# One slot's order on three engines: the exponential ahead of y's tanh, the decay matmul ahead of the gram products, z's gate first and gated y behind N

## The reference

```
y = silu(conv(xn @ W_qkvz))          # q, k, v ; z is taken from the projection, not convolved
beta = sigmoid(b); g = -exp(A_log) * softplus(a + dt_bias)
step: S = S*exp(g); delta = (v - k.S)*beta; S = S + k (x) delta; o = q.S
gated = o * silu(z); gated = rmsnorm(gated) * norm_w ; out = gated @ W_out
```

## Time and profile before

| | |
|---|---|
| median of 3 runs | 3296.51 us (3288.0 to 3297.0) |
| the profiled execution | 3288.43 us, span 3286.7 us |
| mean granted TensorE clock | 0.98 |
| busy, share of the span | PE 92%, weight loads 67%, DVE 71%, ACT 54%, POOL 49% |
| the delta rule's slots | from about 480 us to 2740 us without a break, a slot near 19.8 us |

### The profile page before, as it was taken

How to read it: one execution, slowest core, us unless ns; L and a number is a source line. 1 busy time by engine, 2 the same in 40 slices (tenths; PEclk the granted TensorE clock), 3 DMA queues, 4 the chain that set the end, 5 groups by cost and what they waited for, 6 DMA issues and landing times. The chain is left out here.

```text
span 3286.7 us, 70205 instructions
## 1 busy us (share of the span) xinstructions
PE 3032.7 (92%) x23017; PEld 2186.7 (67%) x23017; DVE 2336.3 (71%) x4933; ACT 1760.5 (54%) x5786; POOL 1621.3 (49%) x3745
## 2 busy tenths in 40 slices
PE   6997699999999999999999999999999999978998
PEld 4555367777767776777677667777776777765555
DVE  3443577777777777777777777777777777755776
ACT  4222466566666666566666666556665666532322
POOL 1000566666666666666666666666666666620000
PEclk9998799999999999999999999999999999987999
DMA  3000111111111111111111111121111111100000
GB/s 74 0 0 20 26 41 37 43 41 44 38 39 40 40 42 36 41 35 42 35 42 35 42 35 42 37 50 37 44 35 42 36 44 36 35 26 22 7 7 13
DMA packets 447056, 113.77 MB, mean 35 GB/s; under 512 B 350496, under 2 KB 445840, under 8 KB 446672
## 3 DMA queue, kind: packets, MB, share of 16 engines
q1 hardware_dynamic: 446672, 108.98, 14.8%
HBM read 63.85 MB, written 45.09 MB: 33 GB/s over the span
## 5 line engine op out<-in xcount | busy, mean ns | idle before, releaser
L876 ACT ACTIVATE raw<-bank 128x512 f32<-128x512 f32 x256 | 153.0, 598 | 433.8 <-PE bank L670 338.7
L467 POOL TENSOR_TENSOR Tb<-Tb,btmp 64x14 f32<-64x14 f32 (+6 forms) x896 | 317.3, 354 | 70.5
L1080 DVE SCALAR_TENSOR_TENSOR N<-ET,ty,bank 128x128 f32<-128x128 f32 x512 | 143.6, 342 | 272.6 <-POOL ET L409 272.6
L1134 DVE SCALAR_TENSOR_TENSOR conv<-raw,ckq,conv 128x512 f32<-128x512 f32 x384 | 308.1, 802 | 26.7 <-ACT conv L877 15.6
L1134 DVE SCALAR_TENSOR_TENSOR conv<-raw,cv,conv 128x512 f32<-128x512 f32 x384 | 312.1, 813 | 14.5 <-ACT conv L877 3.5
L463 POOL TENSOR_TENSOR btmp<-Bk,Tb 64x14 f32<-64x14 f32 (+6 forms) x896 | 274.6, 307 | 65.6
L670 PE MATMUL bank<-xnT,wkq 128*128 128x512 f32 x512 | 254.0, 620 | 42.5 <-ACT ET L831 19.2
L434 POOL TENSOR_TENSOR ty<-ty 128x4 f32<-128x4 f32 x128 | 40.0, 312 | 459.5 <-ACT sq_gat L864 459.5
L670 PE MATMUL bank<-xnT,wv 128*128 128x512 f32 x512 | 249.4, 610 | 11.6 <-issue 7.0
L739 PE MATMUL bank<-wout_h,gT 128*128 128x256 f32 x1024 | 247.8, 385 | 5.2 <-ACT gT L896 5.2
L525 PE MATMUL bank<-S,ykq 128*128 128x256 f32 x1024 | 242.9, 379 | 1.4 <-issue 1.4
(11 more groups left out here) (350 smaller groups left out, 7855.6 us busy)
## 6 DMA issues: line engine op xcount, KB each, us to landing
blk_n<-N SPq DMA_DIRECT2D x128, 256.0 KB, 2.8
Tp<-blk_t SPq DMA_DIRECT2D x128, 128.0 KB, 2.9
Wp<-blk_w SPq DMA_DIRECT2D x128, 128.0 KB, 2.9
wkq<-in_L_attn_W_qkvz_dram SPq DMA_DIRECT2D x32, 128.0 KB, 2.2
wv<-in_L_attn_W_qkvz_dram SPq DMA_DIRECT2D x16, 256.0 KB
Bk<-blk_n SPq DMA_DIRECT2D x64, 64.0 KB, 2.7
blk_t<-Tb SPq DMA_DIRECT2D x64, 64.0 KB, 2.5
blk_w<-Wb SPq DMA_DIRECT2D x64, 64.0 KB, 2.5
```

Source lines behind the costliest of these rows:

```text
L467: pool.tensor_tensor(Tb[:, j + 1:, 0:j], Tb[:, j + 1:, 0:j], tmp, ALU.subtract).then_inc(row_rdy, 1)
L876: act.activation(raw[h][:, j, :, 3:], bB[1 - j], ACT.Copy)
L1080: i = dve.scalar_tensor_tensor(out=N[t.c % RING][:, u, :], in0=ET[:, u, :], scalar=ty[t.c][:, CC, u:u + 1], in1=bB[3][:, u // 2, 0:P], op0 ...
L1134: dve.scalar_tensor_tensor(out=conv[h][:, j], in0=raw[h][:, j, :, k:k + 256], scalar=cw[:, j, k:k + 1], in1=conv[h][:, j], op0=ALU.mult, o ...
```

## The change

Nothing is added or removed; four functions or groups move within a slot. On PE the decay matmul, with its waits, goes ahead of the two gram matmuls, with theirs. On ACT y's tanh goes from first place to behind the exponential. On DVE z's gate goes from third place to first, and y's gate (`silu`) from fifth place to behind `strict`.

```diff
                 def front(s):
                     ...
                     i.then_inc(kq_tp, 1)
+                    pe.wait_ge(gtri_rdy, t.done())
+                    wait(pe, zz_rdy, t.done(4))
+                    ends(pe, s, araw_rdy, t, -1)
+                    pe.matmul(bank[1][:], m["gt"][:], gtri[:].rearrange("p u n -> p (u n)"), start=True,
+                              stop=True).then_inc(dt_mm, 1)
                     wait(pe, N_rdy, t.done(1))
                     wait(pe, attn_rdy, t.done(1))
                     for b in range(B):
                         i = pe.matmul(bB[3][:, b], chunk(y, t, 0, b), ...)
                     i.then_inc(gram_mm, 1)
-                    (the same five lines)
@@ ACT
                 def body(s):
-                    silu(s)
                     ztanh(s)
                     from_state(s)
                     xev64(s)
                     norms(s)
                     expo(s)
+                    silu(s)
                     normed(s)
@@ DVE
                 def body(s):
+                    gate(s)
                     accumulate(s)
                     rhs(s)
-                    gate(s)
                     xev16(s)
-                    silu(s)
                     add_w64(s)
                     add_w1(s)
                     strict(s)
+                    silu(s)
                     uscale(s)
```

More of the change, by code:

```diff
@@ L632, in front @@
                     i.then_inc(gram_mm, 1)
[L633 to L637, removed]
                 def values(s):
```

## The result

The changed kernel takes 3320.92 us (median of 5 runs, 3314.92 to 3324.07) against 3296.51 (5 runs, 3288.0 to 3299.77): ratio 1.0074, 95% interval 1.0056 to 1.0092, so about 24 us slower. The profiled execution took 3320.92 us, 32.5 more than the profiled one of before. The kernel before was timed 47 times more beside the experiments, with medians of 3289.0 to 3291.2 us, so the cost may be nearer to 30 us than to 24.

A forecast was written before the change was run, and what follows sets the result against it. PE, 95% busy, was taken as the bound, each slot set by the chain through ACT, POOL and DVE to apply. A 0, B +0.95 us over 60 pairs, 57 less 4 for zz, gave +53: 3340 us, range 3290 to 3366.

The forecast's parts named there:

- main case: Whole kernel: late blocks from the DMA still hold B slots, so it is slower, 3340 us, own range 3325 to 3362; chance 50.
- blocks early: Rival: Tb is ready 0.7 us sooner, B slots cost only +0.3 us; 3302 us, +5 to +30; chance 24 in 100.
- ACT without y's tanh in front: ACT, slot's front: squares come 1.21 us earlier, at 3.51 us after state_in; the exponential runs at 4.53.
- POOL in the A slot: With y's gate gone, POOL's last base_first instruction shortens from 1.23 us and derive starts at 4.80 instead of 6.01.
- y's gate behind N: DVE, A slot: N at 8.20, the gate adds 1.13 us before Us; state_in to apply 11.11 us against 11.19.
- The B slot: Transposes, 0.85 us late through x16's wait for Tp, now hold the squares; state_in to apply about 11.9 us against 10.94.
- N 1.2 us earlier: Sign on DVE: the prediction is wrong if N doesn't start 1.2 us earlier.
- Does s stay: Transposes' 0.85 us delay by late Tp in B stays: y's gate stretches base_rest by 0.95 to 1.1 of 1.21 gained.
- DVE held by POOL: DVE may lose 0 to 0.4 us where it starts together with POOL; 0.1 us taken in each slot.
- The decay matmul: PE, ahead of the gram products: ends by 4.31 instead of 5.23, project(0) stops waiting 0.37 us; gives nothing by itself.
- z's gate first: DVE: accumulate and rhs come 0.6 us later, costing nothing; the decay matmul's waits for zz go, -4 us.
- the sum's B term: Sum over slot pairs: each B slot grows by 0.95 us, times 60 pairs, 57 us.

The follow-up runs named there:

- experiments two: From the kernel before, only the decay matmul ahead of the gram products and z's gate first on DVE: 3402.36 us, ratio 1.0345.
- experiment four: From the changed kernel, DVE's gate of y back ahead of add_w64, the rest kept: 3291.36 us, ratio 1.0 to the kernel before.

## Why the prediction came out as it did

The direction and the mechanism of the main case were right. The size was too large: 3320.9 lies in the range, but below the main case's own 3325 to 3362. The rival "blocks early", at +5 to +30, fits the difference of the medians (24) but not the cause, since s stayed. Step by step:

- *ACT without y's tanh in front*: squares forecast at 3.51, measured at 3.50; exponential at 4.53, measured at 4.52.
- *POOL in the A slot*: `derive` forecast at 4.80, measured at 4.79. The freed instruction takes 0.28 us. Shown also from the other side: in the two kernels in which y's gate meets `derive` (experiments two and four), one of its instructions is stretched by 0.9 to 1.0 us. The Trainium skill's rule (GPSIMD Engine Reference, Key points) that POOL contends with vector instructions of two SBUF inputs agrees with all of these rows.
- *y's gate behind N*: forecast 1.13 us up to Us, measured 1.13 in A. T in A forecast 11.11, measured 11.10.
- *The B slot*: forecast 11.9, measured 11.94 in the slot shown and 11.88 on the mean. Moving x16 showed by experiment that s is the cause of what B has over A. The sign "N 1.2 us earlier" holds for A alone; in B N comes 0.6 us earlier on the mean (9.46 to 8.88), as the sum for B implied.
- *Does s stay*: yes, 0.78 before and 0.77 after on the mean over all B slots. `base_rest` gave its gain back under y's gate (1.35 us for one instruction of 0.29); with the gate out of it in experiment four, s was 0.61.
- *DVE held by POOL*: 0.1 was taken in each slot; it was 0 in A. In B it was 0.1 on the mean and 0.2 in the slot shown, where gtri was under way and the gate took 1.40 us instead of 1.22.
- *The decay matmul*: nothing, as forecast (ratio 0.9996 alone). *z's gate first*: nothing in the whole change, as forecast, but it was costed without its condition, z's tanh ahead of y's on ACT. Without that it costs 113 us.

**The step that was mis-sized is the sum's B term**, "+0.95" for 60 pairs. T after the change was forecast well; T before it was taken too low. It came from one B slot with T = 10.94, among the shortest, where the mean of all B slots was 11.30, and the allowance for longer ones was too small: late B slots stood at 11.21 on the mean and went to 12.03, +0.82. And the back edge was put at -4 us in all, where one B slot in eight goes from 11.82 to 11.11. I had put those slots into a rival and into the term for zz, and they belonged in the mean. Over all, T grew by 0.58 in B and shrank by 0.04 in A, 0.54 a pair; 64 x 0.54 = 35 us against the forecast 53, and against 32.5 between the two profiled executions. The medians differ by 24.4; the profiled execution of before lay 8 us under its median. The prediction added its 53 us to that low execution and gave the result, rounded to 3340, as the median, which by its own sum would have been 3349; this took 8 us off the miss without a reason in the kernel.

## What to carry to other kernels

Work moved off the front of an in-order engine is only won if it lands in idle time behind the critical instruction: ahead of Us y's gate cost what it had freed, and behind Us, in half of the slots, the same move was worth 1.5% over the kernel before. When a chain is shortened, ask which late input its slack had covered: here the block `Tp` from the DMA, 0.8 us late on the mean in every second slot and nearly free of cost until then (35 of the 50 B slots before had T at 10.93 to 11.15, whatever s was). And average a slot's length over all of its kinds, the loop's edge too, before multiplying.

## What the runs showed of the hardware

While y's gate ran on DVE, with both inputs in SBUF, a POOL instruction that started under it didn't end before it, however small it was: 128x2 elements took 1.17 us and 128x4 took 1.16, where they take 0.20 and 0.23 elsewhere. In the 13 traces, between 500 and 2700 us, 821 POOL instructions start with the gate or under it, and the earliest ends 0.05 us behind the gate's end. The ones that start 0.06 us or more ahead of it, 592 of them, keep their usual length. Under DVE's N and Us, which read one input from a matmul's bank, POOL's instruction on 64x56 kept its length too (0.27 to 0.30 us, 119 in the changed kernel).

The other way round, the gate was longer where a POOL instruction was still under way: 1.23 us where POOL ended 0.15 us into the gate, 1.32 where it ended 0.24 in, and 1.40 where it ended 0.33 in, against 1.22 where it ended within 0.1 us. In these rows the instruction that started later paid; for the gate that was all but about 0.15 us of the overlap.
